# A four-batch convolution-style attention block: a new opening, four diagonal squares by copy, results first on ScalarE

## The reference, cut to what matters

```
B, C, H, W = 4, 128, 32, 32;  N = H * W = 1024;  4 groups of 32 channels
y   = groupnorm(x) * gamma + beta                     # eps 1e-5, per batch and group
qkv = einsum('bchw,dc->bdhw', y, w_qkv) + b_qkv       # three times 128 channels
w   = softmax(q^T k * C**-0.5, axis=-1)               # 1024 x 1024 for each batch
a   = w v
out = x + einsum('bchw,dc->bdhw', a, w_out) + b_out
```

## Time and profile before

| | |
|---|---|
| median of 3 runs | 141.91 us (140.3 to 143.17) |
| the profiled execution | 141.43 us, of it 139.6 us span |
| PE busy | 131.1 us, 94% of the span |
| DVE busy | 99.0 us, 71% |
| ACT busy | 69.8 us, 50% |
| POOL busy | 68.5 us, 49% |
| chain that ended last | PE 72%, DVE 12%, SP queue 7%, ACT 3% |

### The profile page before, as it was taken

How to read it: one execution, slowest core, us unless ns; L and a number is a source line. 1 busy time by engine, 2 the same in 40 slices (tenths; PEclk the granted TensorE clock), 3 DMA queues, 4 the chain that set the end, 5 groups by cost and what they waited for, 6 DMA issues and landing times.

```text
span 139.6 us, 1850 instructions
## 1 busy us (share of the span) xinstructions
PE 131.1 (94%) x573; PEld 90.6 (65%) x573; DVE 99.0 (71%) x189; ACT 69.8 (50%) x126; POOL 68.5 (49%) x75
## 2 busy tenths in 40 slices
PE   7999999999999949999989999999799999899991
PEld 7987677777776625676555656776455576554691
DVE  0489687999999996787786986698866826751211
ACT  3154768775774365644652276575723355850000
POOL 6032165697338647944095667933583345113000
PEclk9999999999999999999999999999999999999999
DMA  4940000000069679980997349963997179812031
GB/s 138 340 198 0 0 5 0 2 0 0 0 134 207 147 155 208 207 228 8 208 204 156 107 97 203 208 170 77 209 204 188 34 168 211 200 68 75 0 113 38
DMA packets 7065, 17.16 MB, mean 123 GB/s; under 512 B 1936, under 2 KB 2192, under 8 KB 7056
## 3 DMA queue, kind: packets, MB, share of 16 engines
q1 hardware_dynamic: 6768, 16.78, 49.3%
q10 hardware_dynamic: 288, 0.27, 0.6%
HBM read 2.36 MB, written 2.10 MB: 32 GB/s over the span
## 4 chain that ended last, share of the span: by engine, by line
PE 72%; DVE 12%; SPq 7%; ACT 3%; issue 2%; DMA 2%; DVEq 0%; ACTq 0%
PE mixed L791 28%; SPq L239 7%; PE scores L747 7%; PE scores L748 7%; PE scores L750 7%; DVE scores L551 6%; PE scores L817 4%; DVE crossed L575 3%; PE turned L764 3%; PE turned L694 3%; ACT probs L388 2%; PE mixed L694 2%; DMA crossed<-crossed 2%; DVE crossed L562 1%; ACT result L408 1%
## 5 line engine op out<-in xcount | busy, mean ns | idle before, releaser
L310 POOL TENSOR_SCALAR probs<-probs,inv_sum 128x1024 f32<-128x1024 f32 x32 | 36.0, 1126 | 48.1 <-DVE inv_sum L556 48.1
L551 DVE TENSOR_SCALAR_CACHE_REDUCE scores<-scores,key_bias 128x1024 f32<-128x1024 f32 x31 | 40.0, 1290 | 14.6 <-PE scores L750 14.4
L388 ACT ACTIVATE probs<-scores,neg_max 128x1024 f32<-128x1024 f32 x32 | 35.7, 1116 | 23.5 <-DVE scores L551 22.7
L791 PE MATMUL mixed<-crossed,v 128*128 128x512 f32 x96 | 44.7, 593 | 2.0 <-DMA crossed<-crossed 2.0
L747 PE MATMUL scores<-y_hi,z_hi 128*128 128x512 f32 x62 | 34.8, 561 | 0.0
L575 DVE STREAM_TRANSPOSE crossed<-probs 128x1024 f32<-128x1024 f32 x24 | 29.7, 1239 | 0.0
L791 PEld LDWEIGHTS mixed<-crossed,v 128*128 128x128 f32 x96 | 17.3, 190 | 16.2 <-issue 15.4
L748 PE MATMUL scores<-y_lo,z_hi 128*128 128x512 f32 x62 | 24.4, 394 | 0.0
L750 PE MATMUL scores<-y_hi,z_lo 128*128 128x512 f32 x62 | 19.2, 391 | 0.0
L747 PEld LDWEIGHTS scores<-y_hi,z_hi 128*128 128x128 f32 x62 | 11.7, 189 | 7.8 <-issue 6.2
L748 PEld LDWEIGHTS scores<-y_lo,z_hi 128*128 128x128 f32 x62 | 11.7, 189 | 7.2 <-issue 5.7
(11 more groups left out here) (148 smaller groups left out, 159.5 us busy)
## 6 DMA issues: line engine op xcount, KB each, us to landing
crossed<-crossed SPq DMA_DIRECT2D x96, 128.0 KB, 2.3
out_dram<-result SPq DMA_DIRECT2D x7, 256.0 KB, 2.5
xs<-in_x_dram SPq DMA_DIRECT2D x2, 512.0 KB, 6.4
xs<-in_x_dram SPq DMA_DIRECT2D x3, 256.0 KB, 5.1
xs<-in_x_dram ACTq DMA_DIRECT2D x1, 256.0 KB, 3.6
ws<-in_weights_dram SPq DMA_DIRECT2D x1, 256.0 KB, 4.0
out_dram<-result SPq DMA_DIRECT2D x2, 128.0 KB, 1.9
vecs<-in_vectors_dram ACTq DMA_DIRECT2D x1, 3.0 KB, 4.2
```

Of the source, the lines that this page charges most:

```text
L310: pool.tensor_scalar(probs[:, i % RING, :], probs[:, i % RING, :], inv_sum[:, i:i + 1], 1.0, ALU.mult, ALU.mult).then_inc(s_probs, 1)
L388: act.activation(probs[:, i % RING, :], scores[:, i % 2, :], ACT.Exp, bias=neg_max[:, i:i + 1], scale=-1.0, accum_out=row_sum[:, i:i + 1]) ...
L551: dve.tensor_scalar(scores[:, i % 2, :], scores[:, i % 2, :], key_bias[:, b % 2, i:i + 1], None, ALU.subtract, ALU.min, accum_out=neg_max[ ...
L791: mm = pe.matmul(bank, v[:, b % 2, k, :], at, start=first, stop=final)
```

## The change

It has three parts.

1. Diagonal squares. Group 1 has 12 swap transfers instead of 16: the four with k = 0, which move a strip within its own partitions, are copied by engines, two by ScalarE (slots 8 and 9, at the end of the slot), two by GpSimd (slots 8 and 10, behind `normalise`). PE waits for all four before its first tile of group 1, and DVE before it flips block 12.
2. Results first. `biased_result` moves from behind the exponentials of its slot to the head of the slot.
3. The opening. Both halves of the first input are loaded in order by the SP queue, then the weights and the vectors. Block 0 uses plain fp32 `fold`, `y` and `first_z` in place of the three fp32r products. The first piece of `y` comes from an input that was centred while the variance was computed. The tail of `fold` moves from DVE to GpSimd. The statistics of batch 0 stand ahead of the turning of the weights on PE. Twelve products with the zero matrix stand ahead of everything in place of ten, two in place of one behind the variances, none in place of three behind the folding, and two behind the first piece of `z`. The copies of the setup vectors stand further up in ScalarE's order. `norm_b` of the later batches becomes a TENSOR_SCALAR with two scalar operands in place of a SCALAR_TENSOR_TENSOR.

```diff
-    SWAP = 16 * SQ * SQ
+    DIAGONAL_SLOTS = {"scalar": {8: 0, 9: 1}, "gpsimd": {8: 2, 10: 3}}
...
+            return sum(16 * (SQ * SQ - (SQ if g == 1 else 0)) for g in SWAPPED if g <= group and g % 2 == group % 2)
+
+        def diagonal_square(of, g):
+            return crossed[32 * g:32 * g + 32, of, g * N:(g + 1) * N]
...
-            sp.dma_start(xs[:, 0, 0:HALF], x_v[0, :, 0:HALF]).then_inc(s_x[0][0], 16)
+            def load_halves(b):
+                for h in range(HALVES):
+                    half = slice(h * HALF, (h + 1) * HALF)
+                    sp.dma_start(xs[:, b, half], x_v[b, :, half]).then_inc(s_x[b][h], 16)
+
+            load_halves(0)
             sp.dma_start(ws[:, :, :], weights.rearrange("p (t c) -> p t c", t=4)).then_inc(s_w, 16)
+            sp.dma_start(vecs[:, :], vectors).then_inc(s_vecs, 16)
+            load_halves(1)
...
-                for k in range(SQ):
+                for k in range(1 if group == 1 else 0, SQ):
...
 (gpsimd)
+            pool.wait_ge(s_fold, 2)
+            pool.tensor_tensor(fold_lo[:, :], fold[:, :], fold_hi[:, :].bitcast(fp32),
+                               ALU.subtract).then_inc(s_fold_lo, 1)
...
+                    if BLOCKS * b + i in DIAGONAL_SLOTS["gpsimd"]:
+                        g = DIAGONAL_SLOTS["gpsimd"][BLOCKS * b + i]
+                        pool.wait_ge(s_flipped, QB)
+                        pool.wait_ge(s_probs, BLOCKS * b + i + 3)
+                        pool.wait_ge(s_rstd, 3)
+                        pool.tensor_copy(diagonal_square(HOME[1], g), diagonal_square(3, g)).then_inc(s_diagonal["gpsimd"], 1)
...
 (scalar)
+            act.activation(fold[:, :], setup[:, SET_G:SET_G + C], ACT.Copy, scale=-SCALE).then_inc(s_fold, 1)
...
+            act.activation(y_hi[:, 0, 0:FIRST], centred, ACT.Identity, scale=norm_a[:, 0:1],
+                           bias=BETA).then_inc(s_y0_hi, 1)
             act.wait_ge(s_z0, 1)
             act.wait_ge(s_setup, 1)
+            act.activation(first_z, mixed[:, 1, 0:FIRST], ACT.Identity, bias=z_bias[:, :]).then_inc(s_z0_full, 1)
...
                 for i in range(BLOCKS):
+                    if i % QB == 3 and BLOCKS * b + i >= 11:
+                        biased_result((BLOCKS * b + i - 11) // QB)
                     if not swapped(BLOCKS * b + i):
...
-                    if i % QB == 3 and BLOCKS * b + i >= 11:
-                        biased_result((BLOCKS * b + i - 11) // QB)
                     if i == (1 if b == 0 else 2) and not last:
                         y_head(b + 1)
+                    if BLOCKS * b + i in DIAGONAL_SLOTS["scalar"]:
+                        g = DIAGONAL_SLOTS["scalar"][BLOCKS * b + i]
+                        act.wait_ge(s_flipped, QB)
+                        act.activation(diagonal_square(HOME[1], g), diagonal_square(3, g),
+                                       ACT.Copy).then_inc(s_diagonal["scalar"], 1)
...
 (vector)
-                    dve.scalar_tensor_tensor(out=norm_b[:, b:b + 1], in0=minus_means[:, b - lo:b - lo + 1],
-                                             scalar=norm_a[:, b:b + 1], in1=BETA, op0=ALU.mult,
-                                             op1=ALU.add).then_inc(s_norm, 1)
+                    dve.tensor_scalar(norm_b[:, b:b + 1], minus_means[:, b - lo:b - lo + 1], norm_a[:, b:b + 1], BETA,
+                                      ALU.mult, ALU.add).then_inc(s_norm, 1)
...
+                if n == 3 * QB:
+                    dve.wait_ge(s_diagonal["scalar"], 2)
+                    dve.wait_ge(s_diagonal["gpsimd"], 2)
...
+            dve.tensor_scalar(centred, xs[:, 0, 0:FIRST], mixed[:, 0, MINUS_MEAN:MINUS_MEAN + 1], None,
+                              ALU.add).then_inc(s_centred, 1)
...
 (tensor)
+                        if group == 1:
+                            pe.wait_ge(s_diagonal["scalar"], 2)
+                            pe.wait_ge(s_diagonal["gpsimd"], 2)
...
-            keep_warm(10)
+            keep_warm(12)
             pe.wait_ge(s_const, 7 + GROUPS)
+            group_means(0, 1, mixed[:, 1, :], mixed[:, 0, :])
             pe.wait_ge(s_w, 16)
             pe.transpose(setup[:, SET_W:SET_W + C], WQ_T, ident[:, :])
             pe.transpose(setup[:, SET_W + C:SET_W + 2 * C], WK_T, ident[:, :]).then_inc(s_w_turned, 1)
-            group_means(0, 1, mixed[:, 1, :], mixed[:, 0, :])
-            keep_warm(1)
             group_variances(0, 1, mixed[:, 1, :])
+            keep_warm(2)
...
+            pe.matmul(mixed[:, 1, first], fold[:, :], y[:, 0, first], start=True, stop=True).then_inc(s_z0, 1)
+            keep_warm(2)
+            pe.wait_ge(s_z0_full, 1)
+            pe.wait_ge(s_y0, 2)
+            pe.matmul(to[0], first_z, y[:, 0, halves[0]], start=True, stop=True)
+            pe.wait_ge(s_y0_rest, 1)
+            pe.matmul(to[1], first_z, y[:, 0, halves[1]], start=True, stop=True).then_inc(s_scores, 1)
```

More of the change, by code:

```diff
@@ L605, in _ @@
             dve.wait_ge(s_vecs, 16)
-            coefficients(0, 1, 1, mixed[:, 0, MINUS_MEAN:MINUS_MEAN + 1])
+            dve.wait_ge(s_rstd, 1)
+            dve.tensor_scalar(norm_a[:, 0:1], rstd[:, 0:1], GAMMA, None, ALU.mult).then_inc(s_scale, 1)
+            dve.wait_ge(s_scale, 1)
+            dve.wait_ge(s_centred, 1)
+            dve.tensor_scalar(y[:, 0, 0:FIRST], centred, norm_a[:, 0:1], BETA, ALU.mult, ALU.add).then_inc(s_y0, 1)
+            dve.scalar_tensor_tensor(out=norm_b[:, 0:1], in0=mixed[:, 0, MINUS_MEAN:MINUS_MEAN + 1],
+                                     scalar=norm_a[:, 0:1], in1=BETA, op0=ALU.mult, op1=ALU.add).then_inc(s_norm, 1)
@@ L608, in _ @@
             dve.wait_ge(s_norm, 1)
-            pieces = (slice(0, FIRST), slice(FIRST, SPLIT))
-            dve.tensor_scalar(y[:, 0, pieces[0]], xs[:, 0, pieces[0]], norm_a[:, 0:1], norm_b[:, 0:1],
+            dve.tensor_scalar(y[:, 0, FIRST:SPLIT], xs[:, 0, FIRST:SPLIT], norm_a[:, 0:1], norm_b[:, 0:1],
                               ALU.mult, ALU.add).then_inc(s_y0, 1)
[L612 to L625, removed]
@@ L626, in _ @@
-            dve.wait_ge(s_setup, 1)
-            first_z_tail(1, mixed[:, 1, 0:FIRST], 0, FIRST)
-            half_stats(1, 1)
+            half_stats(1, 1)
+            for k, piece in enumerate((slice(0, FIRST), slice(FIRST, SPLIT))):
+                dve.wait_ge(s_y0, k + 1)
+                dve.wait_ge(s_y0_hi, k + 1)
+                dve.tensor_tensor(y_lo[:, 0, piece], y[:, 0, piece], y_hi[:, 0, piece].bitcast(fp32),
+                                  ALU.subtract).then_inc(s_y0_lo, 1)
             channel_stats(1, 2)
-            first_z_tail(2, turned[:, 0, FIRST:HALF], FIRST, HALF)
@@ L836, in _ @@
             pe.matmul(setup[:, SET_S:SET_S + 1], ones[:, :], bias_product[:, :], start=True, stop=True).then_inc(s_folded, 1)
-            keep_warm(3)
             first = slice(0, FIRST)
             left = slice(FIRST, HALF)
-            pe.wait_ge(s_norm, 1)
-            pe.wait_ge(s_fold_hi, 1)
-            pe.wait_ge(s_fold_lo, 1)
-            pe.wait_ge(s_y0_hi, 1)
-            pe.matmul(mixed[:, 1, first], fold_hi[:, :], y_hi[:, 0, first], start=True, stop=False)
-            pe.matmul(mixed[:, 1, first], fold_lo[:, :], y_hi[:, 0, first], start=False, stop=False)
@@ L847, in _ @@
-            pe.wait_ge(s_y0_lo, 1)
-            pe.matmul(mixed[:, 1, first], fold_hi[:, :], y_lo[:, 0, first], start=False, stop=True).then_inc(s_z0, 1)
-            pe.wait_ge(s_y0_hi, 2)
+            to = [scores[:, 0, half] for half in halves]
+            pe.wait_ge(s_fold, 2)
+            pe.wait_ge(s_y0, 1)
+            pe.matmul(mixed[:, 1, first], fold[:, :], y[:, 0, first], start=True, stop=True).then_inc(s_z0, 1)
+            keep_warm(2)
+            pe.wait_ge(s_z0_full, 1)
+            pe.wait_ge(s_y0, 2)
@@ L850, in _ @@
+            pe.matmul(to[0], first_z, y[:, 0, halves[0]], start=True, stop=True)
+            pe.wait_ge(s_y0_rest, 1)
+            pe.matmul(to[1], first_z, y[:, 0, halves[1]], start=True, stop=True).then_inc(s_scores, 1)
+            pe.wait_ge(s_y0_hi, 2)
+            pe.wait_ge(s_fold_lo, 1)
             pe.matmul(turned[:, 0, left], fold_hi[:, :], y_hi[:, 0, left], start=True, stop=False)
             pe.matmul(turned[:, 0, left], fold_lo[:, :], y_hi[:, 0, left], start=False, stop=False)
-            to = [scores[:, 0, half] for half in halves]
@@ L853, in _ @@
-            pe.wait_ge(s_z0_hi, 1)
-            pe.matmul(to[0], z_hi[:, 0, first], y_hi[:, 0, halves[0]], start=True, stop=False)
             pe.wait_ge(s_y0_lo, 2)
             pe.matmul(turned[:, 0, left], fold_hi[:, :], y_lo[:, 0, left], start=False, stop=True).then_inc(s_z0, 1)
-            pe.matmul(to[0], z_hi[:, 0, first], y_lo[:, 0, halves[0]], start=False, stop=False)
-            pe.wait_ge(s_y0_hi, 3)
-            pe.matmul(to[1], z_hi[:, 0, first], y_hi[:, 0, halves[1]], start=True, stop=False)
@@ L860, in _ @@
-            pe.wait_ge(s_z0_lo, 1)
```

(7 more changed lines are left out.)

60 lines of the change are left out of this document (32 added, 28 removed).

## The result

| | before | changed |
|---|---|---|
| median of 20 runs | 141.19 us | 141.79 us |
| lowest and highest | 139.73 to 143.17 | 140.73 to 143.54 |
| profiled execution, span | 141.43, 139.6 | 143.54, 141.8 |

The ratio is 1.0078, with a 95% interval of 1.0053 to 1.0103: slower by 0.8%, where 0.2% faster was forecast. The runs differ by the granted clock of PE: of the 20 runs of the changed kernel 3 have a mean clock of 1.00 (140.73, 140.74 and 140.94 us), 16 have 0.988 (median 141.87) and one, the profiled one, has 0.976 (143.54). The profiled execution therefore shows the mechanism, but at more than twice its usual price: it lies 2.8 us above 140.74, the sixteen lie 1.1 us above it.

The account below looks back on a forecast made before the run. PE was taken as the bound, busy 94% of the span, with DVE full from 24 to 51.6 us. Terms -1.57 + 1.4 - 0.15 = -0.3 us against the profiled 141.43 gave 141.1; range 138.6 to 143.6.

Parts of the forecast that it names:

- Diagonal squares: PE's start on group 1: wait for GpSimd's second copy replaces the wait for transfers, PE at 53.0 against 51.59, +1.4 us.
- Results first: Slots 15 and 23: PE's two waits for a result held by ScalarE go, 0.79 + 0.78, -1.57 us.
- The opening: Start to block 1's scores: scores 0 end at 11.8, block 1's begin at 13.4; -0.15 us, between -0.9 and +0.4.
- rival (c): PE's gap before group 1's mixing: clock falls to 1.2 GHz, 2.1 us more, 144.1 us; chance 0.15.
- the slow form of the wait: PE's gap before group 1's mixing with `norm_b` held: idle from 49.56 to 53.9, 4.3 us, squares +2.3.
- the short form: PE's gap before group 1's mixing with `norm_b` not held: idle from 49.56 to 53.0, 3.4 us, squares +1.4.
- The price of 2.1 us: Mixing behind PE's gap at 0.86 us an instruction in place of 0.43 for 4.3 us, if the clock falls: 2.1 us.
- Rival (a): Slot 9 on DVE: `norm_b` is held by GpSimd as today, squares +2.3, sum +0.6, 142.0 us; chance 0.27.

## Why the prediction was wrong

**The sum at a constant clock held; the step that failed is the clock.** The forecast was -0.3 us, 141.1, and its sum has no term for the clock. The three runs of the changed kernel in which the clock stayed have a median of 140.74; the kernel before has 140.93 without its three runs of 142.8 and more. The other 17 runs of the changed kernel have a median of 141.91, 1.2 us higher, and this turns the small gain into a loss of 0.6. I had the fall as rival (c) with a chance of 0.15, and only "in the slow form of the wait", 4.3 us. It came in the short form, 3.56 us, and in 17 runs of 20. I took the longest idle before, 2.04 us, as one that leaves the clock alone, because the profiled execution shows 1.00 there. One execution was no evidence: among 23 later runs of the kernel before, 8 had a mean clock of 0.987 or 0.988 and a median of 142.87, against 141.01 for the other 15. (In two further sets of 17 runs it was none and one; what makes the sets differ is open.) In the run with results first alone the clock fell behind a wait of 2.35 us: 0.59 granted in the window behind.

```profile
51.40:53.00 1.60, 1.55 (x2) 0.63 (x3) 1.57 (x5) 1.34 (x2) 1.60 (x2) 0.59 0.97 210
```

The price of 2.1 us was too high for the usual run and too low for the profiled one: 1.1 us between the groups of the changed kernel (140.74 to 141.87), at most 1.65 us by the median with the gap filled, and 2.6 us in the profiled execution (5.40 - 2.81).

That the sum came so close has luck in it. The terms as the traces show them are -1.9 for the results, +1.5 for the squares and +0.14 for the opening, -0.3 together; against -1.57, +1.4 and -0.15 the first is off by 0.3 one way and the other two by 0.4 the other way.

**Diagonal squares: right.** The new wait is for GpSimd's second copy (forecast 52.9, ended 53.08), PE starts at 53.23 (53.0), the copies take 1.03 to 1.06 (1.1), DVE loses 0.46 us at the flip (at most 0.5), and the wait of 3.6 us lies in the forecast's 3 to 4. Against the first issue PE starts 1.5 us later, +1.4 forecast. That `norm_b` would not be held was right, but the reason given, its new form, decides nothing here: with the old form it isn't held either, because the first copy moves GpSimd's normalisation behind it. I had that shift of 0.1 us in the working ("pushes `normalise` of block 11 (47.23 today) by 0.1") and didn't ask what else it moves past. Rival (a), the held `norm_b`, fell with it.

**Results first: right in kind, under-sized.** 1.57 forecast, 1.9 by start-to-start distances. The term was taken from the list of waits instead of from the starts. The measured ratio of the run with it alone can't tell 1.57 from 1.9.

**The opening: right within its bounds.** -0.15 forecast, between -0.9 and +0.4; the trace shows block 1's scores 0.14 us later, the run with it alone 0.9983 (0.9928 to 1.0037). The scores of block 0 come at 12.3 rather than 11.8, and the means started at 6.32, not at 5.89: the 24 warm-up instructions took 5.49 us, the slow pitch throughout.

## What to carry to other kernels

When a transfer is replaced by copies on engines, write down for each copy which instruction stands ahead of it in its queue and what that one waits for; the last of these sets the time, and here one slot in GpSimd's order was 3 us of the median. A wait of PE that grows can be priced twice, once by its length and once by the clock behind it, so look at the clock of many runs, in more than one set, and not of the profiled one alone. A wait of PE is worth the distance from start to start less the usual pitch, which here is more than the idle time shown (0.95 against 0.79 us).

## What was not expected of the hardware

- PE's granted clock fell in 17 of 20, 8 of 12 and 3 of 6 runs of the kernels with a wait of 3.5 us, and in 8 of 23, 0 of 17 and 1 of 17 runs of the kernel before (2.04 us in its trace). The length alone doesn't decide: the trace with 2.35 us shows a fall, those with 2.48 and 3.51 us show none. In the profiled execution it stood at 1.2 GHz for some 5 us of work. Fourteen products with a zero matrix in the gap kept it at 2.4 GHz in 12 of 12 runs.
- A copy of 32x1024 float32 takes GpSimd 1.03 us and ScalarE 1.04, nearly as long as a pass over 128x1024 (1.12 and 1.12): a quarter of the partitions saves less than a tenth.
- A TENSOR_SCALAR of 128x1 with one SBUF input is not held by a working GpSimd (0.27 us); a SCALAR_TENSOR_TENSOR with two that starts 0.10 us behind GpSimd's instruction is (1.03 us), one that starts 0.10 us ahead of it is not (0.22 us).
